# In layer one of a two-layer graph attention kernel, the first half of each batch's running sums is stored by an indexed DMA that leaves out lanes without a target's end

## The chip, the core and the metric

One core of one Trainium2 chip. The metric is the device time of one launch in microseconds, the median of 3 runs. The engines are named as the profile names them: PE (TensorE), DVE (VectorE), ACT (ScalarE), POOL (GpSimd), SP (SyncE). A DMA that SP issues is on queue q1, one that POOL issues on q0; both run on the same 16 DMA engines.

## The reference, cut to what matters

The input is a graph of 6250 nodes with 256 features and 106,250 edges: 50,000 random pairs in both directions and one loop per node, sorted by target. Layer one of the attention does for each edge and each of 8 heads:

```
feat = (xn @ W1).reshape(nodes, 8, 64)
e = leaky_relu(el[src] + er[dst], 0.2)
ex = exp(e - segment_max(e, dst)[dst])
out = segment_sum(ex / segment_sum(ex, dst)[dst] * feat[src], dst)
```

Then come ELU, layer two of the same kind with one head of 256, a linear attention over all nodes, and eight experts of three matmuls each. Targets have 106250 / 6250 = 17 edges on average, in neighbouring positions of the sorted list.

## The kernel before, in words

**Tiling.** The sorted edges are laid out in 13 groups (Q) of 128 lanes by 64 positions (J). A lane walks along its 64 edges, so a target's edges are summed along one lane's positions. The work goes in 52 batches (NB) of 16 positions (G), four batches per group (PB). `edge_pass` (L1424) runs once for layer one and once for layer two; the linear attention runs beside layer one (class `Mixing`), the experts beside layer two.

**A batch in layer one.** POOL gathers, for each of the 16 positions, one row of 520 floats per lane from the node table into `rows` (L1514), which has two buffers: the gather for position g of batch n waits until step g of batch n-2 has been summed (L1513). DVE's `head(n)` (L1562, first instruction L1565) waits for all 16 gathers of batch n and computes the running maxima; it is called inside batch n-1, ahead of step 12. ACT scales four heads of each position (L1647), DVE the other four of all 16 at once (L1593). Then DVE makes 16 steps: step 0 is L1598, L1601 and L1607, the others are one instruction each (L1624), which multiplies the sum before by `same` (1 if the target is the same as at the position before) and adds the position's row. Every step's sum goes to `ring`, two halves of 8 positions by 528 floats. ACT copies the maxima to the half (L1653).

**Stores.** When the 8 steps of a half are done, SP stores the whole half to the table `sums` in DRAM (L1487), 128 runs of 16,896 bytes, 2112 KB. DVE may write a half again only when its last store has landed: the wait on `stored[0]` is at L1595, ahead of step 0 (L1598), that on `stored[1]` at L1612, ahead of step 8; ACT waits for them at L1652.

**Readers of the sums.** `hidden_pass` (L1667) gathers from `sums` one row per node, the one at the target's last edge, or a merged one. `MergedTails` handles targets that go on in the next lane: in batches with n % 4 = 0 and 1 it has DVE, ACT and PE instructions between the steps, and in batch n % 4 = 2 POOL gathers the rows that are to be merged (`gather`, L1376, DMA L1380) and first waits until every store of the group has landed. No other rows of `sums` are read.

**Order of the queues.** Each engine's program is written out by hand in order. SP: per batch a start table's load (L1470), the first half's loads and stores of the linear attention (L893), the wait for step 8 and the first store, then `tails.sync` (L1363), the second half's, the wait for step 16 and the second store. POOL: 16 gathers per batch, one small gather more in batches n % 4 = 1 ahead of position 8 (L1499) and one in n % 4 = 2 behind position 4 (L1380). `index_pass` (L418) computes all index tables before; there POOL issues 52 scatters (L413) beside DVE's arithmetic.

Of the kernel before, what the change touches and what calls it, by code (L numbers as in the profile page):

```python
# [12 lines left out]
P = 128  # L13
# [24 lines left out]
HALVES = [(0, 8), (8, 16)]  # L38
LENGTH = [c1 - c0 for c0, c1 in HALVES]
# [9 lines left out]
class Layer:  # L49


    def __init__(self, name, heads, width, act_heads, buffers, ahead):
        self.name, self.heads, self.width = name, heads, width
        self.buffers, self.ahead = buffers, ahead
# [8 lines left out]
L1 = Layer("l1", 8, 512, 4, 2, 12)  # L63
L2 = Layer("l2", 1, 256, 1, 3, 14)
# [354 lines left out]
def index_pass(nc, a, k):  # L419
# [3 lines left out]
    with Scope(nc, "at") as s:  # L423
# [58 lines left out]
        last_lane = s.sb("last_lane", [P, P])  # L482
        ends = s.sb("ends", [P, 2, Q])
# [44 lines left out]
        def _(dve):  # L528
# [221 lines left out]
            dve.wait_ge(iota_made, 1)  # L750
            c(V.tensor_copy(at[:, :], at_i[:, :]))
            c.done()
# [564 lines left out]
class MergedTails(Tails):  # L1317
# [58 lines left out]
    def gather(self, pool, q):  # L1376
        pool.wait_ge(self.stored[0], 16 * PB * (q + 1))
        pool.wait_ge(self.stored[1], 16 * PB * (q + 1))
        wait(pool, self.merged, q)
        self.nc.gpsimd.indirect_dma_start(out=self.head[:, :], out_offset=None, in_=self.sums[0:q * RP + CAP, :],  # L1380
# [36 lines left out]
    def sync_out(self, sp, q):  # L1417
        sp.wait_ge(self.merged, q + 1)
        sp.dma_start(self.sums[q * RP + CAP:(q + 1) * RP, :], self.tl[:, :]).then_inc(self.out, 16)
# [4 lines left out]
def edge_pass(nc, a, k, L, work_of):  # L1424
# [4 lines left out]
    with Scope(nc, "e" + L.name[1]) as s:  # L1429
# [6 lines left out]
        ring = s.sb("ring", [P, 2, 8, R])  # L1436
# [13 lines left out]
        dm_ready = s.sems("dm_ready")  # L1450
        stored = s.sems("stored")
# [9 lines left out]
        final = ring[:, 1, LENGTH[1] - 1, :]  # L1461

        @block.sync
        def _(sp):
# [12 lines left out]
            for n in range(NB):  # L1477
# [3 lines left out]
                for i, (c0, c1) in enumerate(HALVES):  # L1481
# [8 lines left out]
            sp.wait_ge(stored[0], 16 * NB)  # L1490
            sp.wait_ge(stored[1], 16 * NB)

        @block.gpsimd
        def _(pool):
# [3 lines left out]
            def first_er(q):  # L1498
                nc.gpsimd.indirect_dma_start(out=er0[:, q, :], out_offset=None, in_=er_table,  # L1499
                                             in_offset=bass.IndirectOffsetOnAxis(ap=k.dst0[:, q:q + 1], axis=0)  # L1500
                                             ).then_inc(er0_in[q % 2], 16)

            first_er(0)
            for n in range(NB):
                for g in range(G):
# [5 lines left out]
                    if n % PB == 1 and g == G // 2 and n // PB + 1 < Q:  # L1511
# [4 lines left out]
                                                 ).then_inc(rows_in[n % B], 16)  # L1516
                    tails.pool(pool, n, g)
                    work.pool(pool, n, g)
            work.pool_last(pool)

        @block.vector
        def _(dve):
# [39 lines left out]
            def head(n):  # L1562
# [14 lines left out]
                wait(dve, dm_ready[1], n - 1)  # L1577
# [9 lines left out]
            for n in range(NB):  # L1587
# [7 lines left out]
                wait(dve, stored[0], n * 16)  # L1595
                wait(dve, summed, n * G)
                if AH < H:
                    c(nc.vector.tensor_tensor(ring[:, 0, 0, 0:W].rearrange(by_head, h=H),  # L1598
                                              ring[:, 1, LENGTH[1] - 1, 0:W].rearrange(by_head, h=H),
                                              broad(share(b)[:, :, 0], dim), ALU.mult))  # L1600
                    c(nc.vector.tensor_tensor(ring[:, 0, 0, W:W + H], ring[:, 1, LENGTH[1] - 1, W:W + H], wr[:, b, :], ALU.mult))  # L1601
                else:
                    c(nc.vector.tensor_scalar(ring[:, 0, 0, 0:W + H], ring[:, 1, LENGTH[1] - 1, 0:W + H], wr[:, b, 0:1], None,
                                              ALU.mult))
                c.done()
                dve.wait_ge(scaled, n * G + 1)
                nc.vector.tensor_tensor(ring[:, 0, 0, 0:W + H], ring[:, 0, 0, 0:W + H], rows[:, rb, 0, 0:W + H], ALU.add  # L1607
                                        ).then_inc(summed, 1)

                for i, (c0, c1) in enumerate(HALVES):  # L1610
                    if i == 1:
                        wait(dve, stored[1], n * 16)  # L1612
                    for j in range(max(c0, 1), c1):
                        if j == L.ahead and n < NB - 1:
                            head(n + 1)
                        er_along(n, j)
                        tails.vector(dve, n, j)
                        work.vector(dve, n, j)
                        if j == G - 1 and n:
                            wait(dve, tails.kept, n // PB)  # L1620
                        prev = ring[:, i, j - c0 - 1, 0:W + H] if j > c0 else ring[:, 1 - i, LENGTH[1 - i] - 1, 0:W + H]
                        dve.wait_ge(scaled, n * G + (j + 1))
                        dve.wait_ge(summed, n * G + j)
                        nc.vector.scalar_tensor_tensor(ring[:, i, j - c0, 0:W + H], prev, k.same[:, n * G + j:n * G + j + 1],  # L1624
# [42 lines left out]
def hidden_pass(nc, a, k):  # L1667
    L = L1
    HB = 3 * KB
    with Scope(nc, "hi") as s:  # L1670
# [29 lines left out]
        def _(pool):  # L1700
# [7 lines left out]
            for n in range(NB):  # L1708
# [5 lines left out]
                if n >= HB:  # L1714
                    scatter(n - HB)
# [703 lines left out]
```

## Time and profile before

| | |
|---|---|
| median of 3 runs | 3247.81 us (3247.24 to 3248.17) |
| span of the profiled execution, first to last instruction | 3526.7 us |
| DVE busy | 2302.8 us (65%) |
| PE busy | 2158.3 us (61%) |
| POOL busy | 2134.4 us (61%) |
| ACT busy | 1906.1 us (54%) |
| DMA | 783.82 MB, mean 222 GB/s |
| steps of layer one | from 346 to 1690 us of the span |

The profiled execution has no time of its own beside the span; it is longer by 278.9 us than the median, and all durations below are its own. Busy time is summed per engine over the whole span, so it says little of one stage; the stages are read from stretches. The page cuts the span into 40 slices of 88 us and gives each engine's busy share as a digit.

### The profile page before, as it was taken

What the parts mean: (1) busy time and instruction counts of PE and PEld (TensorE: products, weight loads), DVE (VectorE), ACT (ScalarE), POOL (GpSimd) and SP (SyncE); (2) the same over time, 40 slices, a digit from 0 to 9 for tenths busy, and PEclk for the clock granted to TensorE, in tenths of its full rate; (3) what the DMA queues carried; (4) which work ended last, traced back from release to release, by engine and by line L of the source; (5) the groups of instructions that cost most, each with busy time, mean ns of one, the idle gap of its engine ahead of it and who ended that gap; (6) DMA issues with size and microseconds to landing.
All of it is one profiled execution on the core that took longest, in us unless ns stands there. A gap on an engine that the chain in (4) does not pass through costs nothing. (4 is left out here: it accounts for less than half of the span.)

```text
span 3526.7 us, 33756 instructions
## 1 busy us (share of the span) xinstructions
PE 2158.3 (61%) x7294; PEld 1353.6 (38%) x7294; DVE 2302.8 (65%) x5558; ACT 1906.1 (54%) x6229; POOL 2134.4 (61%) x2028
## 2 busy tenths in 40 slices
PE   6700455555544454544581006888898888888999
PEld 5600333333333332333361003544454444554565
DVE  7882788888988888888563235655466554665631
ACT  3300778787867667766462224544455444554532
POOL 3337677777767777764475666666666666666200
PEclk9855566666755555555796557989898998989999
DMA  6413899999989999998544465555565555555310
GB/s 230 122 21 103 312 338 345 341 348 337 374 330 364 369 345 358 364 348 318 156 127 116 151 226 186 163 167 177 177 190 160 171 173 174 188 171 169 136 33 12
DMA packets 244661, 783.82 MB, mean 222 GB/s; under 512 B 70282, under 2 KB 118253, under 8 KB 217801
## 3 DMA queue, kind: packets, MB, share of 16 engines
q0 software_dynamic: 127664, 369.53, 33.2%
q1 hardware_dynamic: 86715, 391.15, 29.1%
q10 hardware_dynamic: 30078, 20.99, 2.4%
q8 instruction: 59, 0.97, 0.1%
q14 instruction: 145, 1.19, 0.1%
HBM read 404.26 MB, written 378.13 MB: 222 GB/s over the span
## 5 line engine op out<-in xcount | busy, mean ns | idle before, releaser
L1514 POOL DMA_INDIRECT e_rows<-scratch_table,k_src x1664 | 1742.9, 1047 | 816.0 <-issue 400.3
L1624 DVE SCALAR_TENSOR_TENSOR e_ring<-e_ring,k_same,e_rows 128x520 f32<-128x520 f32 (+1 forms) x1560 | 967.6, 620 | 505.0 <-ACT e_rows L1647 179.0
L1647 ACT ACTIVATE e_rows<-e_rows 128x64 f32<-128x64 f32 (+1 forms) x4160 | 1196.9, 371 | 36.4 <-issue 24.9
L2251 PE MATMUL e_p_y<-e_wfo,e_h 128*121 128x256 f32 x1664 | 418.3, 407 | 116.4 <-DVE e_y L2013 67.6
L2251 PEld LDWEIGHTS e_p_y<-e_wfo,e_h 128*121 128x121 f32 x1664 | 325.8, 198 | 224.9 <-issue 128.5
L2225 PE MATMUL e_p_a<-e_xt,e_wf 128*128 128x484 f32 x832 | 387.4, 611 | 10.2 <-ACT e_h L2160 6.5
L2160 ACT ACTIVATE e_h<-e_p_a,e_shift,e_scale 128x484 f32<-128x484 f32 x208 | 151.9, 749 | 435.0 <-remote 282.5
L2237 PE MATMUL e_p_b<-e_h,e_wf 128*128 128x484 f32 x832 | 362.6, 578 | 13.8 <-ACT e_h L2160 11.5
L2013 DVE SCALAR_TENSOR_TENSOR e_y<-e_p_y,e_w,e_y 121x256 f32<-121x256 f32 x416 | 181.0, 476 | 248.5 <-PE e_p_y L2251 101.1
L1017 PE MATMUL e_p_kv<-e_wkv,nd_feat 128*121 128x512 f32 x208 | 190.0, 1066 | 107.2 <-DVE nd_feat L922 73.5
L1593 DVE TENSOR_TENSOR e_rows<-e_rows,e_shared 128x4096 f32<-128x4096 f32 x52 | 229.7, 4416 | 22.5 <-issue 8.9
L2160 ACT ACTIVATE e_h<-e_p_b,e_shift,e_scale 128x484 f32<-128x484 f32 x208 | 152.3, 749 | 164.8 <-PE e_p_b L2237 76.3
L2225 PEld LDWEIGHTS e_p_a<-e_xt,e_wf 128*128 128x128 f32 x832 | 168.6, 206 | 179.6 <-issue 161.2
L2237 PEld LDWEIGHTS e_p_b<-e_h,e_wf 128*128 128x128 f32 x832 | 154.2, 192 | 183.9 <-issue 173.7
L1053 PE MATMUL e_p_q<-k_ident,e_low 121*128 121x121 f32 x104 | 32.4, 410 | 305.6 <-DVE e_low L948 282.5
L1031 PE MATMUL e_p_c<-e_vext,e_kphi 121*128 121x129 f32 x208 | 63.0, 397 | 163.4 <-ACT e_low L984 99.5
L1639 ACT ACTIVATE e_wr<-e_d 128x8 f32<-128x8 f32 (+1 forms) x104 | 21.2, 204 | 212.6 <-issue 69.0
L1053 PEld LDWEIGHTS e_p_q<-k_ident,e_low 121*128 121x128 f32 x104 | 14.8, 198 | 311.1 <-DVE e_low L948 286.8
L1017 PEld LDWEIGHTS e_p_kv<-e_wkv,nd_feat 128*121 128x121 f32 x208 | 58.0, 309 | 175.3 <-issue 92.9
L1173 PE MATMUL e_p_x<-k_ident,e_fin 128*8 128x128 f32 (+1 forms) x26 | 8.1, 311 | 189.3 <-ACT e_fin L1168 189.3
L219 POOL DMA_INDIRECT na_found<-in_dst,na_piece x52 | 54.8, 1054 | 94.5 <-DVE na_piece L271 94.5
L1031 PEld LDWEIGHTS e_p_c<-e_vext,e_kphi 121*128 121x128 f32 x208 | 45.1, 268 | 172.0 <-ACT e_low L984 107.0
(438 smaller groups left out, 3569.4 us busy)
## 6 DMA issues: line engine op xcount, KB each, us to landing
scratch_rows_a<-e_ring SPq DMA_DIRECT2D x104, 2112.0 KB
scratch_sums<-e_ring SPq DMA_DIRECT2D x104, 1032.0 KB
e_rows<-scratch_table,k_src POOLq DMA_INDIRECT x1664
scratch_table<-na_frow ACTq DMA_DIRECT2D x52, 245.8 KB
scratch_table<-hi_frow ACTq DMA_DIRECT2D x52, 124.8 KB
na_x<-in_x SPq DMA_DIRECT2D x13, 484.0 KB
e_wkv<-in_x SPq DMA_DIRECT2D x52, 121.0 KB
scratch_res<-e_wkv SPq DMA_DIRECT2D x52, 121.0 KB
```

The source lines that it names most:

```text
L219: nc.gpsimd.indirect_dma_start(out=found[:, n % 4, :], out_offset=None, in_=pieces, in_offset=bass.IndirectOffsetOnAxis(ap=piece[:, n:n + ...
L1017: nc.tensor.matmul(self.p_kv[0:BK, :], self.k.feat[:, t, kt, :], self.wkv[:, kt, :], start=kt == 0, stop=kt == 1)
L1031: last = nc.tensor.matmul(self.p_c[:, m * (P + 1):(m + 1) * (P + 1)], part[0:BK, m * P:(m + 1) * P], self.vext[:, m, :], start=False, stop ...
L1514: nc.gpsimd.indirect_dma_start(out=rows[:, n % B, g, :], out_offset=None, in_=table, in_offset=bass.IndirectOffsetOnAxis(ap=k.src[:, n * G ...
L1593: c(nc.vector.tensor_tensor(v, v, broad(share(b)[:, AH:H, 1:G1].rearrange("p h j -> p j h"), dim), ALU.mult))
L1624: nc.vector.scalar_tensor_tensor(ring[:, i, j - c0, 0:W + H], prev, k.same[:, n * G + j:n * G + j + 1], rows[:, rb, j, 0:W + H], ALU.mult, ...
L1647: last = nc.scalar.activation(rows[:, rb, j, at], rows[:, rb, j, at], ACT.Copy, scale=rows[:, rb, j, W + h:W + h + 1])
L2013: last = nc.vector.scalar_tensor_tensor(y, self.p_y[bank][0:BK, i % 2 * D:(i % 2 + 1) * D], self.w[:, i, e:e + 1], y, ALU.mult, ALU.add)
L2160: self.nc.scalar.activation(h[:, e % 2, mt, :], p[mt][:, 0:GN], ACT.Relu, bias=self.shift[:, layer, 2 * e + mt:2 * e + mt + 1], scale=self ...
L2225: last = nc.tensor.matmul(self.p_a[mt][:, 0:GN], self.wf1[:, e, kt, mt * P:(mt + 1) * P], self.xt[:, kt, :], start=kt == 0, stop=kt == 1)
L2237: last = nc.tensor.matmul(self.p_b[mt][:, 0:GN], self.wf2[:, e, kt, mt * P:(mt + 1) * P], self.h1[:, e % 2, kt, :], start=kt == 0, stop=kt ...
L2251: last = nc.tensor.matmul(self.p_y[bank][0:BK, i * D:(i + 1) * D], self.h2[:, e % 2, kt, v:v + BK], self.wfo[:, e, kt, :], start=kt == 0, ...
```

## The change

The first half of each batch in layer one is no longer stored by SP. POOL stores it with an indirect DMA: each lane's 8 sums, 16,896 bytes, go to the row that an index table names, and a lane whose index is out of bounds is left out. The index of a run of 8 positions is its home row, plus 4,000,000 if none of the 8 positions is the last of its target in the lane. The second half is stored as before. The index table is computed once, in `index_pass`. POOL issues the store of batch n-2 right behind its gather for position 0 of batch n, and waits there until the 8 steps and the copy of the maxima are done; the last two are issued after all gathers. DRAM and SBUF operands of these DMAs are written as int32 (the same bytes). Layer two keeps both stores on SP. The rest of the diff renames and reorders without another effect on the work (`ring` is addressed by slot, the loop over DVE's steps is flat).

```diff
+            nc.gpsimd.iota(home_i[:, :], [[RP // HB, Q], [1, HQ]], base=0, channel_multiplier=HQ).then_inc(iota_made, 1)
...
+            c(V.tensor_copy(home[:, :], home_i[:, :]))
...
+            c(V.tensor_reduce(inner_steps[:, :], other[:, :, :].rearrange(line).rearrange("p (u s) -> p u s", s=HB),
+                              AX.X, ALU.add))
+            c.done()
+            c(V.memset(inner_steps[0:1, 0:1], 0.0))
+            c.done()
+            c(V.tensor_scalar(inner_steps[:, :], inner_steps[:, :], HB - 0.5, NONE, ALU.is_gt, ALU.mult))
+            c.done()
+            c(V.tensor_tensor(k.half[:, :], home[:, :], inner_steps[:, :], ALU.add))
...
     def gather(self, pool, q):
-        pool.wait_ge(self.stored[0], 16 * PB * (q + 1))
-        pool.wait_ge(self.stored[1], 16 * PB * (q + 1))
+        for i, done in enumerate(self.stored):
+            pool.wait_ge(done, 16 * self.L.stores(HQ * (q + 1), i))
...
+        def filled(eng, u):
+            eng.wait_ge(summed, (u + 1) * HB)
+            eng.wait_ge(dm_ready[L.slot(u)], L.turns(u) + 1)
...
-                for i, (c0, c1) in enumerate(HALVES):
+                for i in range(2):
                     if i == 1:
                         tails.sync(sp, n)
                     work.sync(sp, n, i)
-                    sp.wait_ge(summed, n * G + c1)
-                    sp.wait_ge(dm_ready[i], n + 1)
-                    sp.dma_start(out[n // PB][:, n % PB * G + c0:n % PB * G + c1, :], ring[:, i, 0:c1 - c0, :]).then_inc(stored[i], 16)
+                    if L is L2 or i == 1:
+                        u, at = 2 * n + i, n % PB * G + i * HB
+                        filled(sp, u)
+                        run = ring[:, L.slot(u), :, :]
+                        sp.dma_start(out[n // PB][:, at:at + HB, :], run.bitcast(I32) if L is L1 else run
+                                     ).then_inc(stored[L.slot(u)], 16)
...
+            homes = sums.rearrange("(u s) r -> u (s r)", s=HB)
+
+            def store(u):
+                filled(pool, u)
+                nc.gpsimd.indirect_dma_start(
+                    out=homes, out_offset=bass.IndirectOffsetOnAxis(ap=k.half[:, u:u + 1], axis=0),
+                    in_=ring[:, L.slot(u), :, :].rearrange("p s r -> p (s r)").bitcast(I32), in_offset=None,
+                    bounds_check=Q * RP // HB - 1, oob_is_err=False).then_inc(stored[L.slot(u)], 16)
...
+                    at = n * G + g - STORE_AT
+                    if L is L1 and at >= 0 and at % G == 0:
+                        store(at // HB)
                     tails.pool(pool, n, g)
                     work.pool(pool, n, g)
+            if L is L1:
+                for n in range((T - 1 - STORE_AT) // G + 1, NB):
+                    store(2 * n)
...
-                wait(dve, dm_ready[1], n - 1)
+                last = 2 * (n - 2) + 1
+                if last > 0:
+                    dve.wait_ge(dm_ready[L.slot(last)], L.turns(last) + 1)
```

## Rows read from the trace of the kernel before

**Rows 1.** The page: the span, and the busy tenths of the DMA engines.
```profile
span 3526.7 us, 33756 instructions
...
DMA  6413899999989999998544465555565555555310
```

**Rows 2.** Groups of instructions on VectorE in layer one, 346 to 1690 us.
```profile
L1624 DVE SCALAR_TENSOR_TENSOR e_ring<-e_ring,k_same,e_rows 128x520 f32<-128x520 f32 x780 | 589.9, 756 | 127.9 <-ACT e_rows L1647 38.7 <-DMA na_x<-in_x 34.3 <-issue 5.2
L1593 DVE TENSOR_TENSOR e_rows<-e_rows,e_shared 128x4096 f32<-128x4096 f32 x51 | 225.2, 4416 | 20.3 <-ACT e_rows L1640 7.3 <-issue 6.7 <-DMA na_x<-in_x 3.4
```

**Rows 3.** Waits of VectorE, same stretch: line, releaser, us in total, times, longest.
```profile
DVE e_ring L1624 <- ACT e_rows L1647: 38.7, 58, 5.6
DVE e_ring L1624 <- DMA na_x<-in_x: 34.3, 13, 9.7
DVE e_den L944 <- remote: 17.9, 3, 6.0
DVE e_den L944 <- PE e_p_kv L1046: 15.0, 14, 1.6
```

**Rows 4.** Windows by stage: the whole layer, then batches 12, 13 and 14.
```profile
core 0: us, PE busy (x) PEld busy (x) DVE busy (x) ACT busy (x) POOL busy (x), PEclk, DMA share, GB/s
346.00:1690.00 1344.00, 679.88 (x2088) 433.94 (x2088) 1129.74 (x2063) 1001.12 (x4044) 925.13 (x831) 0.60 0.92 344
659.80:692.10 32.30, 15.60 (x49) 10.24 (x49) 23.59 (x45) 22.97 (x90) 19.33 (x19) 0.64 0.82 287
692.10:715.40 23.30, 13.20 (x40) 8.09 (x40) 21.84 (x40) 19.75 (x82) 17.26 (x15) 0.71 0.96 360
715.40:738.30 22.90, 13.85 (x40) 8.58 (x40) 20.89 (x40) 18.94 (x78) 18.02 (x17) 0.61 1.01 385
```

**Rows 5.** DMA queues in 346 to 1690 us: packets, MB, share of the 16 engines.
```profile
DMA packets 98404, 462.22 MB, mean 344 GB/s; under 512 B 17058, under 2 KB 29642, under 8 KB 85070
...
q0 software_dynamic: 65998, 218.49, 46.3%
q1 hardware_dynamic: 32320, 242.89, 45.8%
...
scratch_rows_a<-e_ring SPq DMA_DIRECT2D x104, 2112.0 KB
```

**Rows 6.** Groups of instructions on GpSimd, the same stretch, and an indexed store elsewhere.
```profile
L1514 POOL DMA_INDIRECT e_rows<-scratch_table,k_src x808 | 901.1, 1115 | 366.5 <-issue 172.1 <-DVE e_ring L1624 114.6 <-DVE e_ring L1607 79.7
...
L413 POOL DMA_INDIRECT scratch_starts<-nd_er,k_index x52 | 60.7, 1167 | 77.9 <-DVE at_ones L732 62.3 <-issue 15.5
```

**Rows 7.** Timeline of VectorE, batches 22 and 23: start, us, instruction, idle before.
```profile
925.99 0.74 DVE L1624 SCALAR_TENSOR_TENSOR e_ring<-e_ring,k_same,e_rows 128x520 f32<-128x520 f32 x1
...
940.70 0.68 DVE L1598 TENSOR_TENSOR e_ring<-e_ring,e_shared 128x512 f32<-128x512 f32 x1
...
951.76 0.38 DVE L1565 TENSOR_TENSOR e_z<-e_rows,e_er 128x128 f32<-128x128 f32 x1
```

**Rows 8.** Timeline of SyncE from 920 us: the store of a first half.
```profile
926.76 47.02 SPq L1487 DMA_DIRECT2D scratch_rows_a<-e_ring  x5
```

**Rows 9.** Timeline of GpSimd, the gathers round the start of batch 25.
```profile
941.79 1.21 POOL L1514 DMA_INDIRECT e_rows<-scratch_table,k_src  x1 [0.30 <-issue]
...
954.21 0.94 POOL L1514 DMA_INDIRECT e_rows<-scratch_table,k_src  x1 [0.30 <-issue]
955.46 1.26 POOL L1499 DMA_INDIRECT e_er<-scratch_er,k_dst  x1 [0.30 <-issue]
```

**Rows 10.** Timeline: the end of the index pass, then the first gathers of layer one.
```profile
256.54 0.15 DVE L818 SCALAR_TENSOR_TENSOR k_slot<-k_iota,at_p_s 128x13 int32<-128x13 f32 x1
...
300.76 1.01 POOL L413 DMA_INDIRECT scratch_starts<-nd_er,k_index  x1 [0.30 <-issue]
...
333.15 0.94 POOL L1514 DMA_INDIRECT e_rows<-scratch_table,k_src  x1 [0.30 <-issue]
...
336.91 0.42 DVE L1565 TENSOR_TENSOR e_z<-e_rows,e_er 128x128 f32<-128x128 f32 x1 [14.01 <-DMA e_rows<-scratch_table,k_src]
```

More of the change, by code:

```diff
@@ L37 @@
 CW = 2 * (P + 1)
-HALVES = [(0, 8), (8, 16)]
-LENGTH = [c1 - c0 for c0, c1 in HALVES]
+HB = 8
+NH = T // HB
+HQ = NH // Q
+STORE_AT = 32
 GB = 13
@@ L60, in __init__, with slot, turns, stores @@
         self.act_heads = act_heads
-L1 = Layer("l1", 8, 512, 4, 2, 12)
-L2 = Layer("l2", 1, 256, 1, 3, 14)
+    def slot(self, u):
+        return u % self.halves
+    def turns(self, u):
+        return u // self.halves
+    def stores(self, u, slot):
+        return (u - slot + self.halves - 1) // self.halves
+L1 = Layer("l1", 8, 512, 4, 2, 12, 2)
+L2 = Layer("l2", 1, 256, 1, 3, 14, 2)
 def wait(eng, sem, value):
@@ L1605, in _ @@
                 c.done()
                 dve.wait_ge(scaled, n * G + 1)
-                nc.vector.tensor_tensor(ring[:, 0, 0, 0:W + H], ring[:, 0, 0, 0:W + H], rows[:, rb, 0, 0:W + H], ALU.add
+                nc.vector.tensor_tensor(first[:, 0:W + H], first[:, 0:W + H], rows[:, rb, 0, 0:W + H], ALU.add
                                         ).then_inc(summed, 1)
[L1610 to L1624, printed above, removed]
-                                                       rows[:, rb, j, 0:W + H], ALU.mult, ALU.add).then_inc(summed, 1)
@@ new lines, in _ @@
+                for j in range(1, G):
+                    if j == HB:
+                        wait(dve, stored[L.slot(2 * n + 1)], 16 * L.turns(2 * n + 1))
+                    if j == L.ahead and n < NB - 1:
+                        head(n + 1)
+                    er_along(n, j)
+                    tails.vector(dve, n, j)
+                    work.vector(dve, n, j)
+                    if j == G - 1 and n:
+                        wait(dve, tails.kept, n // PB)
+                    t = n * G + j
+                    dve.wait_ge(scaled, t + 1)
+                    dve.wait_ge(summed, t)
+                    nc.vector.scalar_tensor_tensor(row(t)[:, 0:W + H], row(t - 1)[:, 0:W + H], k.same[:, t:t + 1],
+                                                   rows[:, rb, j, 0:W + H], ALU.mult, ALU.add).then_inc(summed, 1)
@@ L1642, in _ @@
                 act.wait_ge(wr_ready, n + 1)
-                for i, (c0, c1) in enumerate(HALVES):
+                for i in range(2):
+                    u, c0, c1 = 2 * n + i, i * HB, (i + 1) * HB
                     for j in range(c0, c1):
@@ L1673, in hidden_pass @@
         prod = s.sb("prod", [P, 4, D])
-        rows = s.sb("rows", [BK, HB, L.row])
+        rows = s.sb("rows", [BK, RB_, L.row])
         rec = s.sb("rec", [BK, 2, KB, 8])
@@ L1708, in _ @@
             for n in range(NB):
-                b = n % HB
-                wait(pool, agg_ready, n - HB + 1)
-                nc.gpsimd.indirect_dma_start(out=rows[:, b, :], out_offset=None, in_=k.sums1,
+                b = n % RB_
+                wait(pool, agg_ready, n - RB_ + 1)
+                nc.gpsimd.indirect_dma_start(out=rows[:, b, :].bitcast(I32), out_offset=None, in_=k.sums1,
                                              in_offset=bass.IndirectOffsetOnAxis(ap=k.index[:, 1, n:n + 1], axis=0)
                                              ).then_inc(rows_in[b], 16)
-                if n >= HB:
-                    scatter(n - HB)
-            for n in range(NB - HB, NB):
+                if n >= RB_:
+                    scatter(n - RB_)
+            for n in range(NB - RB_, NB):
                 scatter(n)
```

57 lines of the change are left out of this document (30 added, 27 removed).

## The prediction

> **What bounds the kernel now.** I read the page first, for the stage. The DMA engines are at nine tenths in slices 5 to 19 and nowhere else for long [rows 1]; that is layer one, whose steps run from 346 to 1690 us. Then the groups and waits of that stretch, to see which engine's work is never free. DVE is busy 1129.7 of 1344 us [rows 4]; its 780 steps at 756 ns follow each other [rows 2]. Its four largest waits make 105.9 us together: for ACT's scaling, for a matmul of the linear attention (one by name, one that the view calls remote), and 34.3 us under the name of a load that ended two stages earlier, so a name the view doesn't resolve [rows 3]. None is named after a store or a gather, and the longest is 9.7 us. So in the profiled execution DVE sets the pace, with PE and ACT giving it short stalls, mostly in the batch that carries the merging (32 us instead of 23 [rows 4]).
>
> The reader should see two engines right behind it. The DMA share is 0.92 on average, and in a 23 us batch it is 0.96 to 1.01 at 360 to 385 GB/s [rows 4]: the rings are full, and only slack keeps this from DVE. The slack of a store: the steps of batch 22's first half end at 926.73, SP issues at 926.76 [rows 8], and DVE writes the half again at 940.70 [rows 7], 13.9 us later. The slack of the gathers: the last for batch 24 is issued from 941.79 to 943.00 (the ninth back from the small gather at 955.46, which stands ahead of position 8 [rows 9]); `head(24)` starts at 951.76 [rows 7], 8.8 us later, without waiting. POOL is the second: a gather lasts 1.115 us on average with 0.30 us to the next [rows 6, 9], so 832 + 24 of them at 1.415 us fill 1211 of the 1344 us.
>
> **The change part by part.** The sum goes against the profiled span of 3526.7 us; the medians are 278.9 us lower, and I carry the difference over to 3247.8 unscaled.
>
> Bytes left out: with 17 edges per target, a run of 8 positions holds no last edge for 17 - 8 = 9 of 17 starting places (few targets have fewer than 8 edges, as the degree is 1 plus about 16 with a spread of 4), 0.53 of the lanes. That is 52 x 128 x 0.53 = 3528 runs of 16.9 KB, 59.6 MB of 462.2 [rows 5]. Queue q1 spends 45.8% of 1344 us on 242.9 MB [rows 5], 2.53 us per MB, so the DMA engines lose 151 us of work and their share falls from 0.92 to 0.81. On the path in the profiled execution: nothing, since no wait of DVE ends with a store [rows 3]. The Trainium skill ("DMA: Bandwidth & Descriptors", section Bandwidth) says that transfers between HBM and SBUF are bound by the HBM side, about 358 GB/s per core. By that rule the stage is at its ceiling and the bytes left out would be worth 59.6 / 358, an estimate of 166 us; batch 14 runs above that figure [rows 4], which differs from the page.
>
> SP's part: 52 waits and issues go, and the loads and stores of the linear attention behind them are no longer held for step 8. They wait for ACT's results anyway. Zero; if that cover is gone it can only be a gain, of under 1 us a batch.
>
> The index table: one iota and a copy, a reduction over 832 elements, and three small operations, under 3 us of DVE (4.4 us for 4096 elements in L1593 [rows 2], so 0.9 for 832; the small ones like L818's 0.15 us [rows 10]). DVE is done with the pass at 256.54, POOL's scatters go on past 300 [rows 10]. Hidden by 45 us. Zero.
>
> POOL's new issue: no indexed store of 16.9 KB runs is in the trace. The nearest row by kind is the scatter of 32 bytes from 121 lanes, 1.167 us [rows 6]; the nearest by size is the gather, 1.115 us for 2 KB per lane [rows 6]. If a run is one piece, as in SP's store, the issue is like these: 1.15 + 0.30 = 1.45 us, 75 us in 52 batches. If runs are cut into pieces of the gather's size, it is eight gathers, 8.9 us. Below 1.45 nothing. I take 1.45, the row of the same kind. POOL has 1344 - 1211 = 133 us free, so 75 fit; per batch POOL then needs 16.5 + 1 issues, about 24.7 us, against a mean of 25.8.
>
> POOL's new wait is the term that counts. It stands behind position 0 of batch n and ends with step 8 of batch n-2; queued behind it are gathers 1 to 15, which now may start with steps 1 to 15, and for them waits `head(n)`. For batch 24: the wait ends at 926.73 [rows 7], the store starts at 927.03, gather 1 at 928.48, gather 15 at 928.48 + 14 x 1.415 = 948.3 and ends at 949.4, instead of 943.0. That is 6.4 us later, and 2.4 us are left to `head` at 951.76. How long does a gather take to land? The first batch's last gather is issued until 334.09 and `head(0)`, which waits for it, starts at 336.91 [rows 10]: 2.8 us, ahead of the stage's first store. From above, a whole store of 2112 KB ahead of it at 344 GB/s [rows 5] adds 6.3: 9.1 us. I take 4, near the lower end, as the share falls to 0.81 and the store in the way is halved. Then `head` waits 4 - 2.4 = 1.6 us. In the batches ahead of the merging batch this holds in the first half of the stage, 6 times, 10 us. The other batches of a group are longer before `head` or have POOL earlier (the small gathers and the attention's tail), and in the second half a full batch is longer; I take them at zero, and give back 1 us for SP. With a landing of 2.8 us the stall is 0.4 us and the sum 2; with 9.1 it is 6.7 us in every group and some in the batches between, 13 x 6.7 = 87. Sum: 10 - 1 = **+9 us**, 3257.
>
> The store itself starts when it did before and moves half as much: 1.45 for the issue, 2.8 to land, 3.0 for about 1 MB at 344 GB/s, 7.3 of a 13.9 us slack. What is late next is this one: POOL falls behind by 24.7 - 23 = 1.7 us in each of three short batches, 5 us, still under the 6.6 left.
>
> **Rivals.** *The DMA engines bind in the timed runs (faster).* For: they are full in three batches of four [rows 4], and the timed runs are shorter than the profiled one. If this stage is shorter in the same ratio (0.921), it is 1238 us, 373 GB/s, which is what the full batches reach. Then leaving out 59.6 MB pays until POOL stops it: 1211 + 75 = 1286 us, at 0.921 1184, a gain of 54; if POOL's durations don't shrink, none. I price it at -43: 3205. Against: POOL's issue interval need not be shorter there, and the 279 us may lie in other stages. 0.29.
>
> *All of the stage goes with its bytes.* Then 59.6 MB at the stage's 344 GB/s [rows 4] are 173 us: 3075. The stage would be 1171 us, just above DVE's busy time of 1130. But nothing on DVE waits for a store [rows 3], so 0.03. This is what the Trainium skill's ceiling ("DMA: Bandwidth & Descriptors", Bandwidth) comes to here.
>
> *POOL becomes the bound (slower).* Place: the issue of the indexed store, between gathers 0 and 1. It decides from the point where 16.5 x 1.415 + x exceeds 25.8, x over 2.5 us. At 4 us it costs 52 x 1.5 = 78: 3326. At 8.9 it would be 330. For: nothing here shows a large run in a software queue. Against: the scatter's 1.167. 0.14.
>
> *Nothing happens:* lanes are left out but gathers land within 2.4 us, or hardly any lane is left out and POOL's delay is hidden anyway: within 3 us of 3248. 0.16. The forecast has 0.38.
>
> **How the numbers follow.** About 0.2%, 6.5 us, is what a measurement of this kernel can tell from no change. The forecast's case runs from 0 to +25; a third of it (0.13) lies within 6.5. Faster: 0.29 + 0.03 = 0.32. Same: 0.16 + 0.13 = 0.29. Slower: 0.25 + 0.14 = 0.39. Cases of both signs hold most of the chance: the forecast's own range is 3248 to 3273. The range for 8 in 10 leaves out the case by bytes and the dear end of the POOL rival: from 3193 (a gain of 54 to 55) to 3335 (the forecast's 87 us with the slow landing, which takes in the POOL rival at 4 us).
>
> **What would show it.** Right: in the changed profile DVE's L1565 waits for the gathers in some batches, 1 to 2 us each; the indexed store lasts about 1.15 us on POOL and its wait appears as POOL idle of 4 to 6 us per batch; DMA bytes in the stage fall by about 60 MB and the share to near 0.8; DVE's busy time is unchanged. Wrong: a stage that is shorter with DVE's waits for PE and ACT smaller; a store of over 2.5 us on POOL; waits of DVE's L1598 for the first half's store; a drop of bytes far from 60 MB.

## The result and the profile after

The changed kernel takes **3271.1 us** (median of 4 runs, 3267.16 to 3272.33) against 3247.52 us for the kernel before: ratio 1.0073 with a 95% interval of 1.0059 to 1.0086, 23.6 us slower. The forecast was 3257 in a range of 3193 to 3335, with slower as the likeliest outcome (0.39).

One plain fact comes first, because it decides how the rows ahead of the prediction are to be read: the profiled execution of the kernel before that they come from was 279 us longer than that kernel's timed runs. A second profile of the same kernel (label b0) has a span that agrees with them. VectorE is busy as long in both, 2302.8 and 2303.2 us, so the first execution has 279 us more of waiting, 68 of them in layer one (below); why, no run here shows. "Undisturbed" means an execution like the second. From here on, "before" in a comparison means that second profile.

The page after, its first lines and its DMA queues:

```profile
span 3268.2 us, 33814 instructions
...
DMA  7611888899888999999745476666666666666410
...
DMA packets 244661, 723.99 MB, mean 222 GB/s; under 512 B 73824, under 2 KB 121795, under 8 KB 221343
...
q0 software_dynamic: 135152, 422.16, 42.0%
q1 hardware_dynamic: 79227, 278.69, 23.0%
```

The bytes fell from 783.82 to 723.99 MB, 59.8 MB less. The tenths in the slices of layer one fell from mostly nine [rows 1] to eights and nines.

How long is layer one? VectorE's first instruction of step 0 runs once per batch, so the distance from its first to its last start is 51 batches. The answers for that source line, first the profile of before read ahead of the prediction, then the second one, then after:

```profile
L1598 DVE TENSOR_TENSOR e_ring<-e_ring,e_shared x52: 677/680/683, 345.8 to 1669.8; 128x512 f32<-128x512 f32 x52
```
```profile
core 0 of [0], span 3244.6 us
...
L1598 DVE TENSOR_TENSOR e_ring<-e_ring,e_shared x52: 677/679/681, 351.1 to 1606.9; 128x512 f32<-128x512 f32 x52
```
```profile
L1651 DVE TENSOR_TENSOR e_ring<-e_ring,e_shared x52: 678/680/684, 347.5 to 1628.6; 128x512 f32<-128x512 f32 x52
```

That is 1324.0, 1255.8 and 1281.1 us, or 25.96, 24.62 and 25.12 us per batch. After less before is 25.3 us, the whole of the measured 23.6 and a little more: all of it is in layer one. And the mean batch of an undisturbed execution is 1.3 us shorter than the one the prediction was reckoned against.

Where in layer one? Step 0 of batch 2 starts at 401.14 us before and at 395.44 after. That of batch 26, halfway through, before and after:

```profile
968.05 0.68 DVE L1598 TENSOR_TENSOR e_ring<-e_ring,e_shared 128x512 f32<-128x512 f32 x1
```
```profile
989.11 0.68 DVE L1651 TENSOR_TENSOR e_ring<-e_ring,e_shared 128x512 f32<-128x512 f32 x1
```

The 24 batches 2 to 25 take 593.7 us instead of 566.9, 24.74 a batch instead of 23.62: 26.8 us more. The 25 batches from 26 to 50 take 639.5 instead of 638.9, 25.6 a batch in both kernels. Batches 0 and 1 are 2.2 us shorter together. So the whole loss is in the first half of the layer, where the batches are short.

What does VectorE wait for there? Its waits for DMAs from 380 to 1650 us (the first two batches, where everything waits for the first gathers, are left out), before and after. Columns: line, what it waited for, us in total, times, longest:

```profile
DVE e_z L1565 <- DMA e_rows<-scratch_table,k_src: 2.0, 1, 2.0
```
```profile
DVE e_z L1615 <- DMA e_rows<-scratch_table,k_src: 33.5, 16, 3.2
```

L1615 is the first instruction of `head(n)`, L1565 before. It used to find its 16 gathers landed; now it waits for them in 16 batches, about 2 us each, and 15 of the 16 (30.9 us) lie between 380 and 975 us, ahead of batch 26. The waits for PE and ACT, from 340 to 1650 us, shrank a little, by 28.8 + 26.7 - 26.5 - 22.1 = 6.9 us:

```profile
DVE e_den L944 <- PE e_p_kv L1046: 28.8, 22, 3.1
DVE e_ring L1624 <- ACT e_rows L1647: 26.7, 66, 1.0
```
```profile
DVE e_den L970 <- PE e_p_kv L1072: 26.5, 20, 3.1
DVE e_ring L1674 <- ACT e_rows L1698: 22.1, 53, 1.0
```

GpSimd's groups from 350 to 1620 us, before and after:

```profile
L1514 POOL DMA_INDIRECT e_rows<-scratch_table,k_src x808 | 909.8, 1126 | 291.7 <-issue 156.6 <-DVE e_ring L1624 88.7 <-DVE e_ring L1607 46.3
L1499 POOL DMA_INDIRECT e_er<-scratch_er,k_dst x12 | 12.3, 1024 | 3.7 <-issue 3.7
L1380 POOL DMA_INDIRECT e_head<-scratch_rows_a,k_slot x12 | 11.9, 994 | 3.7 <-issue 3.7
```
```profile
L1558 POOL DMA_INDIRECT e_rows<-scratch_table,k_src x806 | 890.1, 1104 | 245.6 <-issue 161.2 <-DVE e_ring L1674 77.4 <-DVE e_ring L1658 4.3
L1542 POOL DMA_INDIRECT scratch_rows_a<-e_ring,k_half x51 | 54.6, 1070 | 41.9 <-ACT e_ring L1704 24.3 <-issue 10.3 <-DVE e_ring L1674 7.3
L1406 POOL DMA_INDIRECT e_head<-scratch_rows_a,k_slot x12 | 15.9, 1329 | 3.7 <-issue 2.1 <-DMA scratch_rows_a<-e_ring,k_half 1.5
L1534 POOL DMA_INDIRECT e_er<-scratch_er,k_dst x11 | 10.4, 945 | 3.4 <-issue 3.4
```

L1542 is the indexed store, 1.07 us each. Its idle time, 41.9 us over 51, is 0.82 us each and not the 4 to 6 us that the prediction wanted to see. Before, GpSimd was busy 934.0 us in 832 issues; with the 0.30 us between two issues [rows 9] that is 1.423 us per issue, 23.5 us for the 16.5 issues of a batch. After, 971.0 us in 880 issues make 1.403, and 17.5 of them 24.6. Both must be held against the batches of each half. GpSimd's gathers before, in batches 2 to 25 and then in 26 to 50:

```profile
L1514 POOL DMA_INDIRECT e_rows<-scratch_table,k_src x387 | 434.9, 1124 | 117.9 <-issue 75.9 <-DVE e_ring L1624 39.6 <-DVE e_ring L1607 2.4
```
```profile
L1514 POOL DMA_INDIRECT e_rows<-scratch_table,k_src x387 | 437.1, 1130 | 163.4 <-issue 72.5 <-DVE e_ring L1624 47.0 <-DVE e_ring L1607 43.9
```

The gathers and the store after, in batches 2 to 25:

```profile
L1558 POOL DMA_INDIRECT e_rows<-scratch_table,k_src x387 | 425.4, 1099 | 117.9 <-issue 73.4 <-DVE e_ring L1674 39.6 <-DVE e_ring L1658 3.3
L1542 POOL DMA_INDIRECT scratch_rows_a<-e_ring,k_half x24 | 27.2, 1133 | 7.3 <-issue 7.3
```

In batches 2 to 25, 117.9 us of idle time over 387 gathers is 0.305 us each, the bare gap: already in the kernel before, GpSimd issued back to back there and had nothing to give. It needed 23.5 us for a batch that took 23.62. Its free time lay in the second half (163.4 us of idle time instead of the 118 of the gaps, about 46 us), where the batches of 25.6 us hold 24.6 us of issues as well. With one issue more, the first half runs at GpSimd's 24.6 (24.74 measured), and the second half does not change. The batch grows by 1.12 us and not by the store's whole 1.133 + 0.305 = 1.44, as the gathers are 0.025 us shorter each. The store's idle time in this half is 7.3 / 24 = 0.30 us, again the bare gap: GpSimd reaches the store after step 8 is done, and the new wait never stops it there.

One of the waits, on GpSimd's timeline and then on VectorE's (start, duration, instruction, idle before it):

```profile
972.68 0.95 POOL L1558 DMA_INDIRECT e_rows<-scratch_table,k_src  x1 [0.30 <-DVE e_ring L1674]
973.93 1.20 POOL L1558 DMA_INDIRECT e_rows<-scratch_table,k_src  x1 [0.30 <-issue]
975.44 1.01 POOL L1542 DMA_INDIRECT scratch_rows_a<-e_ring,k_half  x1 [0.30 <-issue]
```
```profile
971.83 2.48 DVE L1674 SCALAR_TENSOR_TENSOR e_ring<-e_ring,k_same,e_rows 128x520 f32<-128x520 f32 x3
976.93 0.39 DVE L1615 TENSOR_TENSOR e_z<-e_rows,e_er 128x128 f32<-128x128 f32 x1 [2.62 <-DMA e_rows<-scratch_table,k_src]
```

The gather issued from 972.68 to 973.63 is the last of its batch (the next, at 973.93, is position 0 of the following one, with the store behind it). `head` starts at 976.93, 3.3 us after the end of that issue, having stood idle for 2.62 us.

### The profile page after: what moved, and what is told of

It is laid out like the page before. It is cut to its first block and busy times, and to the rows that moved or that the text cites. A ratio compares the mean times of both kernels' runs of the same rounds, so it can differ in the third digit from the quotient of the medians.

```text
span 3268.2 us, 33814 instructions
## 1 busy us (share of the span) xinstructions
PE 2097.5 (64%) x7294; PEld 1328.6 (41%) x7294; DVE 2308.2 (71%) x5563; ACT 1900.5 (58%) x6229; POOL 2173.2 (66%) x2081
## 2 busy tenths in 40 slices
DMA packets 244661, 723.99 MB, mean 222 GB/s; under 512 B 73824, under 2 KB 121795, under 8 KB 221343
## 5 line engine op out<-in xcount | busy, mean ns | idle before, releaser
L1558 POOL DMA_INDIRECT e_rows<-scratch_table,k_src x1664 | 1724.3, 1036 | 506.9 <-issue 362.5
L2301 PE MATMUL e_p_y<-e_wfo,e_h 128*121 128x256 f32 x1664 | 396.5, 394 | 51.8 <-DVE e_y L2063 51.8
L2301 PEld LDWEIGHTS e_p_y<-e_wfo,e_h 128*121 128x121 f32 x1664 | 316.0, 191 | 150.6 <-issue 64.8
L2287 PE MATMUL e_p_b<-e_h,e_wf 128*128 128x484 f32 x832 | 360.3, 576 | 13.9 <-ACT e_h L2210 13.8
L2275 PE MATMUL e_p_a<-e_xt,e_wf 128*128 128x484 f32 x832 | 357.4, 572 | 0.7 <-ACT e_xt L2225 0.7
L2275 PEld LDWEIGHTS e_p_a<-e_xt,e_wf 128*128 128x128 f32 x832 | 157.6, 191 | 146.2 <-issue 140.7
L396 PE MATMUL na_p_f<-na_w,nd_feat 128*121 128x264 f32 x416 | 106.5, 401 | 7.9 <-ACT nd_feat L356 7.9
L427 POOL DMA_INDIRECT scratch_starts<-nd_er,k_index x52 | 59.6, 1147 | 77.7 <-DVE at_ones L750 62.1
```

The costliest lines, as they stand in the source:

```text
L396: last = nc.tensor.matmul(p_f[b][h][0:BK, 0:D + 8], k.feat[:, n, kt, :], w1[:, kt, h, :], start=kt == 0, stop=kt == 1)
L427: nc.gpsimd.indirect_dma_start(out=starts, out_offset=bass.IndirectOffsetOnAxis(ap=k.index[:, 0, n:n + 1], axis=0), in_=k.er[:, n, 0:width ...
L1558: nc.gpsimd.indirect_dma_start(out=rows[:, n % B, g, :], out_offset=None, in_=table, in_offset=bass.IndirectOffsetOnAxis(ap=k.src[:, n * G ...
L2275: last = nc.tensor.matmul(self.p_a[mt][:, 0:GN], self.wf1[:, e, kt, mt * P:(mt + 1) * P], self.xt[:, kt, :], start=kt == 0, stop=kt == 1)
L2287: last = nc.tensor.matmul(self.p_b[mt][:, 0:GN], self.wf2[:, e, kt, mt * P:(mt + 1) * P], self.h1[:, e % 2, kt, :], start=kt == 0, stop=kt ...
L2301: last = nc.tensor.matmul(self.p_y[bank][0:BK, i * D:(i + 1) * D], self.h2[:, e % 2, kt, v:v + BK], self.wfo[:, e, kt, :], start=kt == 0, ...
```

## The experiments

The theories put to the test: **Issue:** GpSimd has no room for one more instruction per batch in the first half of the layer. **Wait:** the new wait for step 8 holds gathers 1 to 15 back. **Bytes:** the DMA engines bind, so that the 60 MB are a gain that hides part of a larger loss, or none. Differences in us below are a kernel's median less that of the kernel before run beside it.

**b0, the kernel before unchanged.**

> The kernel before, unchanged, for a second profile. The first profile's span was 279 us longer than the timed runs, while the changed kernel's span (3268 us) agrees with its timed runs. Expected: a span near 3246 us, so layer one is shorter than the 1341 us of the first profile; if the changed kernel's layer one (1297 us) is 24 us too long, it is near 1273 us here. DVE has no wait for gathers. If layer one is 1340 us again, the difference between the kernels lies elsewhere.

Measured: 3245.11 against 3246.78, ratio 0.9997 (0.9987 to 1.0007). Its profile is the one used above. Its DMA queues from 352 to 1625 us, and the same stretch after (packets, MB, share of the 16 engines):

```profile
DMA packets 98296, 461.12 MB, mean 362 GB/s; under 512 B 17018, under 2 KB 29602, under 8 KB 85026
...
q1 hardware_dynamic: 32256, 241.81, 48.1%
q0 software_dynamic: 65954, 218.46, 47.8%
```
```profile
DMA packets 97581, 397.21 MB, mean 312 GB/s; under 512 B 20411, under 2 KB 32753, under 8 KB 88049
...
q0 software_dynamic: 73137, 269.45, 63.5%
q1 hardware_dynamic: 24360, 126.94, 25.9%
```

The DMA share falls from 0.96 to 0.89, and not to 0.81 as forecast. The premise of the "DMA engines bind" rival holds: an undisturbed layer moves 362 GB/s and the engines are 0.96 full. Whether they bind is for the kernels below.

**e_wait, the wait alone.** GpSimd waits for step 8 where the change waits, and issues nothing; SP stores both halves.

```diff
-                    if L is L2 or i == 1:
+                    if True:
...
             def store(u):
                 filled(pool, u)
-                nc.gpsimd.indirect_dma_start(
...
```

> POOL waits for the 8 steps behind gather 0 as in the changed kernel, but issues no store; SP stores both halves whole, as before. Theory (the wait ahead of gathers 1 to 15 makes them late): DVE's waits for the gathers stay, 20 to 40 us, and the time is 15 to 30 us above the kernel before. Rival (the cost is POOL's extra issue, or the store in the gathers' ring): within 5 us of the kernel before.

Measured: 3253.11 against 3246.78, ratio 1.0019 (1.0010 to 1.0028), 6.3 us. VectorE's wait for gathers from 380 us on:

```profile
DVE e_z L1608 <- DMA e_rows<-scratch_table,k_src: 12.5, 6, 3.2
```

The wait alone costs something near the prediction's term of 10 us, far from 24 and below the 15 to 30 expected. It is not the main cause.

**x_one and x_two, the issue alone.** To the kernel before, one small gather per batch is added on GpSimd (32 bytes per lane, its result never read), ahead of position 10; in x_two there are two, ahead of positions 4 and 12. The diff is x_one's. Nothing waits for a step, and hardly any bytes are added.

```diff
+                    if L is L1 and g in (10,):
+                        wait(pool, spare_in, 16 * (1 * n + (10,).index(g)))
+                        nc.gpsimd.indirect_dma_start(out=spare[:, :], out_offset=None, in_=er_table,
...
```

> The kernel before plus one small indirect gather per batch on POOL (32 bytes per lane, into a tile that nobody reads), ahead of position 10; no new wait for a step. Theory, formed after the first four runs (POOL's issue time is the bound once it has 17 issues per batch: at 1.41 us apart, 52 more are 73 us, and the undisturbed profile of before leaves POOL about 50 us): 15 to 35 us above before, that is nearly all of the changed kernel's 24 us. Rival (the changed kernel's cost is its wait for step 8 and the large store): within 6 us of before.

> The kernel before plus two such small gathers per batch. Theory (POOL bound): past the free time each further issue costs its whole 1.4 us, so 60 to 85 us above the run with one, 80 to 115 us above before. Rival (POOL isn't the bound): under 20 us above before.

Measured: x_one 3275.62 against 3245.42, ratio 1.0091 (1.0078 to 1.0104), 30.2 us. x_two 3315.77, ratio 1.0206 (1.0186 to 1.0226), 70.4 us by the medians and 67 by the ratio. x_one's wait for gathers from 380 us on, then its added issues among GpSimd's groups:

```profile
DVE e_z L1574 <- DMA e_rows<-scratch_table,k_src: 27.3, 8, 6.5
```
```profile
L1517 POOL DMA_INDIRECT e_spare<-scratch_er,k_dst x51 | 54.3, 1064 | 15.5 <-issue 15.5
```

The same for x_two, with the first and last start of its step 0 between them, and all of its GpSimd groups from 350 to 1620 us:

```profile
DVE e_z L1574 <- DMA e_rows<-scratch_table,k_src: 78.5, 18, 7.6
```
```profile
L1607 DVE TENSOR_TENSOR e_ring<-e_ring,e_shared x52: 678/680/683, 351.9 to 1676.0; 128x512 f32<-128x512 f32 x52
```
```profile
L1521 POOL DMA_INDIRECT e_rows<-scratch_table,k_src x786 | 862.7, 1098 | 239.5 <-issue 161.2 <-DVE e_ring L1633 75.3 <-DVE e_ring L1616 3.0
L1517 POOL DMA_INDIRECT e_spare<-scratch_er,k_dst x98 | 105.3, 1074 | 29.8 <-issue 29.8
L1501 POOL DMA_INDIRECT e_er<-scratch_er,k_dst x12 | 13.3, 1107 | 3.7 <-issue 3.7
L1380 POOL DMA_INDIRECT e_head<-scratch_rows_a,k_slot x12 | 13.3, 1106 | 3.7 <-issue 3.4 <-DMA scratch_rows_a<-e_ring 0.3
```

One instruction that moves next to nothing costs as much as the whole change. With two, the expectation (80 to 115 us above before, 60 to 85 above x_one) was missed: 70.4, and 40 above x_one. In x_two GpSimd is the bound outright: its idle time is 276.7 us, of which 908 x 0.30 = 272.4 are the fixed gaps, so it waits for nobody. Busy 994.6 us in 908 issues plus 0.30 is 1.395 us, 25.8 for the 18.5 of a batch, and the batch measures 1324.1 / 51 = 25.96. The second issue cost 40 us; a full 1.395 in each batch would be 73. The difference is the second half of the layer, whose batches grow only from 25.6 to 25.84 us: up to there the issues still fit.

**a_15 and b_15, one issue taken away.** The gather of position 15 is left out from batch 2 on, in the changed kernel and in the kernel before; the sums then use an old row in its place, so these two serve only to take the time apart.

```diff
-                for g in range(G):
+                for g in range(G - 1 if L is L1 and n >= 2 else G):
...
-                dve.wait_ge(rows_in[n % B], (n // B + 1) * 16 * G)
+                dve.wait_ge(rows_in[n % B], (n // B + 1) * 16 * G - (16 * (n // B) if L is L1 else 0))
```

> The changed kernel with the gather for position 15 left out from batch 2 on, so that POOL has 16 issues per batch again, with the indexed store and its wait still there. The row of position 15 is then an old one; 26 MB fewer are read. Theory (POOL bound): 20 us or more below the changed kernel, at or below the kernel before. Rival (the wait for step 8 makes the gathers late whatever the number of issues): within 8 us of the changed kernel.

> The kernel before with the gather for position 15 left out from batch 2 on, so that POOL has 15 issues per batch; 13 MB for each 100 gathers' worth aside, nothing else differs. If POOL already holds the kernel before back in its short batches: 5 to 20 us below before. If POOL was wholly hidden there and only a 17th issue brings it out: within 5 us of before.

Measured: a_15 3248.86 against 3245.42, ratio 1.0013 (1.0005 to 1.0022), 3.4 us; b_15 3244.01 against 3246.63, ratio 0.9991 (0.9981 to 1.0000). a_15's wait for gathers from 380 us on, and its indexed store among GpSimd's groups from 380 to 1560 us; below them the same group of the changed kernel:

```profile
DVE e_z L1615 <- DMA e_rows<-scratch_table,k_src: 5.3, 6, 1.1
```
```profile
L1542 POOL DMA_INDIRECT scratch_rows_a<-e_ring,k_half x48 | 56.9, 1186 | 65.8 <-ACT e_ring L1704 43.9 <-DVE e_ring L1674 14.8 <-issue 7.1
```
```profile
L1542 POOL DMA_INDIRECT scratch_rows_a<-e_ring,k_half x47 | 50.5, 1074 | 35.8 <-ACT e_ring L1704 18.4 <-issue 10.0 <-DVE e_ring L1674 7.3
```

With 16.5 issues per batch again, and the indexed store and its wait still in place, 20 of the 23.6 us are gone. Over both halves GpSimd now arrives earlier at the store: it is idle there for 65.8 / 48 = 1.37 us, the gap of 0.30 included, instead of 35.8 / 47 = 0.76. In the kernel before the same edit changes next to nothing. In batches 2 to 25 it gives GpSimd 29 us of idle time beyond the gaps, but the batch goes only from 23.62 to 23.52 us. So something else, VectorE by its few waits, allows no shorter batch there, and GpSimd in the kernel before just kept up with it. The missing gather also moves 50 x 128 rows of 2080 bytes, 13 MB, less (not the 26 MB of the expectation); b_15, which moves as much less, gains 2.6 us with bytes and issue together.

**e_all32, the change without its gain.** No lane is left out, so the bytes are those of before.

```diff
-            c(V.tensor_scalar(inner_steps[:, :], inner_steps[:, :], HB - 0.5, NONE, ALU.is_gt, ALU.mult))
+            c(V.tensor_scalar(inner_steps[:, :], inner_steps[:, :], HB - 0.5, 0.0, ALU.is_gt, ALU.mult))
```

> The changed kernel with no lane left out: POOL stores all 128 runs of the first half, at the same place. Theory (bytes are off the path): within 8 us of the changed kernel, with some more waiting for the gathers, as they land later. Rival (the bytes left out give back time in the changed kernel): 30 us or more above it. The DMA share of layer one rises by about 11 points, and its bytes by 60 MB.

Measured: 3274.65 against 3246.78, ratio 1.0086 (1.0072 to 1.0100), 27.9 us. DMA from 352 to 1625 us, and the wait for gathers:

```profile
DMA packets 97586, 456.01 MB, mean 358 GB/s; under 512 B 16933, under 2 KB 29275, under 8 KB 84573
...
q0 software_dynamic: 73141, 328.24, 71.8%
q1 hardware_dynamic: 24360, 126.94, 24.7%
```
```profile
DVE e_z L1615 <- DMA e_rows<-scratch_table,k_src: 38.0, 21, 3.3
```

Leaving out 59 MB is worth 27.9 - 23.6 = 4.3 us by the medians, the two intervals overlap, and in the profiles the 51 batches of the layer take 1281.4 us here and 1281.1 in the changed kernel. So in the changed kernel the bytes give nothing that can be told from zero. Their DMA share is 71.8 + 24.7 = 96.5% here, 7 points above the changed kernel's and not the 11 expected.

**e_at39, e_all39 and e_at35, the place of the store.** `STORE_AT = 39` puts it behind gather 7, where GpSimd waits for step 8 in any case; e_all39 leaves out no lane beside that; 35 puts it behind gather 3.

```diff
-STORE_AT = 32
+STORE_AT = 39
```

> The changed kernel with the store issued behind gather 7, whose own wait is already for step 8, so POOL gets no new wait but keeps the issue and the lanes left out. Theory (the wait): DVE's waits for the gathers fall from 36 us to under 12 and the time is 15 to 30 us below the changed kernel, near the kernel before or a little under it. Rival (issue or ring): within 8 us of the changed kernel.

> The store behind gather 7 with no lane left out. With the lanes left out DVE waited 36.6 us for the store to land in this place. Here twice the bytes must land: if the landing is set by the bytes, 30 to 100 us above the run with lanes left out; if it is set by POOL's late issue alone, within 15 us of it.

> The changed kernel with the store behind gather 3, between the two places tried. POOL has the same 17 issues. Theory (POOL bound, the place only decides which wait of DVE shows it): 10 to 40 us above before like both others, with DVE's waits split between the gathers and the landing of the first half's store. Rival (there is a place that hides the issue): within 6 us of before.

Measured: e_at39 3286.89 against 3246.78, ratio 1.0125 (1.0110 to 1.0141); e_all39 3286.43 against 3245.42, ratio 1.0123 (1.0107 to 1.0139); e_at35 3273.18 against 3246.63, ratio 1.0077 (1.0064 to 1.0091). VectorE's waits for DMAs from 380 us on, in this order:

```profile
DVE e_ring L1651 <- DMA scratch_rows_a<-e_ring,k_half: 36.6, 9, 9.1
DVE e_z L1615 <- DMA e_rows<-scratch_table,k_src: 2.8, 3, 1.3
```
```profile
DVE e_ring L1651 <- DMA scratch_rows_a<-e_ring,k_half: 37.0, 19, 10.4
```
```profile
DVE e_z L1615 <- DMA e_rows<-scratch_table,k_src: 42.6, 21, 3.5
```

At 39 no step is waited for that was not waited for before, and the kernel is still 16 us slower than the changed one: the expectation fell. The gathers are in time, but the store starts so late that VectorE's step 0 waits for its landing. In the profiles (3278.79 us for e_at39, its fastest run, 3270.1 for the changed kernel) most of the difference is in batches 0 and 1, which take 54.4 us instead of 47.9. Half the bytes or all of them, the price is the same (40.1 and 41.0 us). At 35 the time came as expected, but not the split of the waits: all of them are for the gathers. The place of the store decides only which of VectorE's waits shows that GpSimd is late.

**b_move.** In the kernel before, the small gather of n % 4 = 1 goes to the next batch.

```diff
-                    if n % PB == 1 and g == G // 2 and n // PB + 1 < Q:
+                    if n % PB == 2 and g == G // 2 and n // PB + 1 < Q:
```

> The kernel before with the small gather of batches n % 4 = 1 issued in n % 4 = 2, behind which DVE is in its longest batch. If POOL's issues hold the short batches back, moving 12 of them gives 2 to 8 us; if POOL is hidden, no change within 3 us.

Measured: 3246.04 against 3246.63, ratio 0.9994 (0.9985 to 1.0003). No change; it says only that it does not matter to the time which of the two batches carries that issue.

None of these beats the kernel before by more than a measurement can tell.

The column on VectorE's waits is of 380 to 1650 us (e_all39's is 37.0 for the store and 3.9 for gathers; its 9.0 us behind second-half stores are not in it); it orders the kernels nearly as the times do.

| kernel | issues per batch | bytes left out | new wait | VectorE's DMA waits on gathers and first-half stores | against before, us |
|---|---|---|---|---|---|
| b0 | 16.5 | no | no | 2.0 | -1.7 |
| b_15 | 15.5 | 13 MB | no | 0 | -2.6 |
| b_move | 16.5 | no | no | 0 | -0.6 |
| a_15 | 16.5 | 60 + 13 MB | yes | 5.3 | +3.4 |
| e_wait | 16.5 | no | yes | 12.5 | +6.3 |
| after | 17.5 | 60 MB | yes | 33.5 | +23.6 |
| e_all32 | 17.5 | no | yes | 38.0 | +27.9 |
| x_one | 17.5 | no | no | 27.3 | +30.2 |
| e_at35 | 17.5 | 60 MB | yes | 42.6 | +26.5 |
| e_at39 | 17.5 | 60 MB | no | 39.4 | +40.1 |
| e_all39 | 17.5 | no | no | 40.9 | +41.0 |
| x_two | 18.5 | no | no | 78.5 | +70.4 |

The same kernels by half of the layer. "Needed" is issues per batch times the mean duration of an issue in batches 2 to 25 plus the gap of 0.304 us; "free" is GpSimd's idle time beyond those gaps.

| kernel | issues per batch | needed, us | batches 2 to 25: us per batch | free, us | batches 26 to 50: us per batch | free, us |
|---|---|---|---|---|---|---|
| b_15 | 15.5 | 22.2 | 23.52 | 29.3 | 25.55 | 76.1 |
| b0 | 16.5 | 23.5 | 23.62 | 0.2 | 25.55 | 45.7 |
| b_move | 16.5 | 23.5 | 23.61 | 0.2 | 25.59 | 44.6 |
| a_15 | 16.5 | 23.5 | 23.70 | 2.7 | 25.62 | 55.7 |
| e_wait | 16.5 | 23.3 | 23.87 | 15.7 | 25.62 | 58.4 |
| after | 17.5 | 24.6 | 24.74 | 0.2 | 25.58 | 26.6 |
| e_all32 | 17.5 | 24.6 | 24.77 | 0.2 | 25.56 | 23.2 |
| x_one | 17.5 | 24.6 | 24.61 | 0.2 | 25.60 | 18.0 |
| e_at35 | 17.5 | 24.8 | 24.93 | 0.2 | 25.62 | 27.0 |
| e_at39 | 17.5 | 24.7 | 24.90 | 3.6 | 25.58 | 35.3 |
| e_all39 | 17.5 | 24.7 | 24.84 | 2.8 | 25.77 | 35.3 |
| x_two | 18.5 | 26.0 | 25.91 | 0.2 | 25.84 | 0.2 |

Wherever GpSimd has nothing free, the batch is what its issues need, within 0.15 us, whether the added instruction is the store or a small gather, with the new wait or without, with the bytes left out or not.

## Why the prediction was right, and what it mis-sized

- **What was right, and what was luck:** the measured 3271 lies in the range and on the side called likeliest (0.39), but the range reached 55 us down and 87 up from the kernel before. The +9 was added up from the new wait. In the changed kernel the wait stops GpSimd nowhere in the first half, and the cost comes from a term that was priced at nothing. The side was right in good part by luck. What did hold is that the last gathers are what VectorE waits for, and that the second half of the layer pays nothing.
- **Bytes:** 59.6 MB forecast, 59.8 measured. That they would pay nothing on the path held (e_all32). Their share of the DMA engines did not fall to 0.81 but to 0.89.
- **The store's issue:** taken at 1.45 us with its gap from the scatter's row [rows 6]; it measures 1.07 + 0.30 = 1.37. The upper bound, a run cut into pieces, did not come true: from 352 to 1625 us, 97581 - 88049 = 9532 packets are of 8 KB or more; SP's 51 stores of 128 runs account for 6528, which leaves 3004 for the indexed stores, 0.46 of their 51 x 128 lanes: one packet per run that is stored. Over the whole execution 73824 - 70282 = 3542 packets more are under 512 bytes than before: one for each lane left out, 0.53 of 52 x 128, as forecast, and 3542 x 16,896 bytes are the 59.8 MB.
- **Where it hurts:** as forecast, `head` waits for the last gathers, 2.1 us a time against 1.6 forecast, and in the first half of the layer, but there in 15 batches instead of 6. GpSimd's idle time at the store, forecast at 4 to 6 us, is 0.8, and 0.3 in that half.
- **The step that failed** is "POOL has 1344 - 1211 = 133 us free, so 75 fit; per batch POOL then needs 16.5 + 1 issues, about 24.7 us, against a mean of 25.8". The 24.7 is right (24.6 measured), the comparison is not. First, the 25.8 came from an execution 279 us too long; an undisturbed batch is 24.62 us. Second, a mean over the layer hides two halves: 23.62 us a batch, where 24.6 do not fit, and 25.6, where they do. The prediction saw that POOL falls 1.7 us behind in each of three short batches, and stopped counting there, as if the 32 us of the fourth [rows 4] let it catch up. Undisturbed, the fourth takes 25.3 (22.0, 23.8, 25.3 and 23.1 us are four batches in a row), so POOL never catches up. Free time there was 0.2 us, and 46 in the second half, where it serves nothing. (The 133 us also count 856 issues, where the stretch holds 831 [rows 4]; that error is to the safe side.) The term costed at nothing is the largest: x_one shows 30 us for an issue without any wait for a step, and a_15 takes 20 of the 23.6 us back by taking one issue away. The wait is 6 us by itself (e_wait), and the terms do not add up, because an engine that is late passes the wait without stopping: beyond its gaps GpSimd idles 15.7 us in batches 2 to 25 of e_wait, and 0.2 in those of the changed kernel.
- **The POOL rival** had the place right and its threshold wrong: by its own formula, with 24.62 in place of 25.8, it decides at an x of about 1.15 us and not 2.5, and x was 1.37. By the mean that would still be only 11 us; with the 23.62 of the first half it decides at almost nothing. With rows of an undisturbed execution, taken by halves of the layer, it would have deserved far more than 0.14.
- **The DMA rival (faster)** was right about the timed stage (1256 us instead of 1324, 362 GB/s, share 0.96) and wrong about what follows. Its gain of 43 us never appears: with GpSimd late, the bytes give nothing that can be told from zero, and in the kernel before 13 MB less (b_15) gives 2.6 us at an interval that reaches zero. The prediction also had the loss in its own figures: a stage of 1238 us in which POOL needs 1286 and does not get faster is not a gain of "none" but 48 us lost. The Trainium skill's ceiling of about 358 GB/s per core ("DMA: Bandwidth & Descriptors", Bandwidth) would have made the layer DMA-bound at its 362. Batches 2 to 25 even ran at 372 GB/s, above that figure, and VectorE had one wait for a gather in them, 2.0 us, and none for a store: being full did not make the DMA engines what the layer waits for. What 60 MB less would bring without any new GpSimd instruction wasn't tried.

## What to carry to other kernels

Before slack is read off a profile, compare its span with the timed runs; slack of 1 us per batch can't be trusted in a trace whose batches are 1.3 us too long. Then count the instructions of the engine that issues the indirect DMAs, times issue plus gap, against the batch, and do it by stretch: an engine that shows 73% busy (934 of 1270 us) was 95% occupied with its gaps over the layer (23.5 of 24.62) and fully occupied in its first half. Slack in one stretch does not pay for another. Saving bytes that nothing waits for with an instruction on such an engine lost time in every form tried here.

## What the runs showed of the hardware beyond that

- **An indirect DMA's issue on GpSimd hardly depends on its bytes** (means over the layer; single ones take 0.94 to 1.64 us)**:** 1.06 us for 32 bytes per lane (x_one), 1.10 for 2 KB (the gathers after), 1.07 for 16.9 KB with half of the lanes left out, 1.08 with none left out (e_all32: 54.9 us in 51). Leaving lanes out saves DMA work and none of GpSimd's. Nor does it save packets: all three executions, before, after and e_all32, have 244661, and after has 3542 more of them under 512 bytes. The Trainium skill ("DMA: Bandwidth & Descriptors", SWDGE vs HWDGE vs iDMA) says that for such a DMA software on a core of GpSimd works out the descriptors, and recommends SP for plain stores ("Issuing engine by pattern"); the trace agrees in that moving a store from SP to GpSimd is what cost the time.
- **The DMA share fell less than the bytes:** 13.9% fewer bytes (461.12 to 397.21 MB) took the share only from 0.96 to 0.89, 7%. The software queue's share per MB rose from 47.8 / 218.46 = 0.219% to 63.5 / 269.45 = 0.236%. In e_all32, where no lane is left out, it is 71.8 / 328.24 = 0.219% again, so the rise comes with the lanes left out and not with the long runs; by what, is open.
